# State scans on one Trainium2 core: D products at every second state, and three of four B chunks as products in one step of four instead of in half of the steps

## The reference

```
def step(h, inp):
    x_t, dt_t, B_t, C_t = inp
    A_bar = jnp.exp(dt_t[..., None] * A)
    h = A_bar * h + dt_t[..., None] * B_t[:, None, :] * x_t[..., None]
    y_t = jnp.einsum('bdn,bn->bd', h, C_t)
    return (h, y_t)
...
return y + D * x
```

## Time and profile before

| | us |
|---|---|
| median of 3 runs | 686.62 |
| lowest, highest | 686.56, 692.63 |
| span of the profiled execution, first to last instruction | 657.3 |
| TensorE busy in it | 602.7 |
| VectorE busy | 530.2 |
| ScalarE busy | 513.7 |
| GpSimd busy | 429.1 |

### The profile page before, as it was taken

The page is one execution under the profiler, slowest core; times in us unless marked ns, Lnnn a source line. Parts: engine busy times, 40 slices in busy tenths (PEclk is TensorE's granted clock), DMA queues, the critical chain, the costliest instruction groups (busy, mean ns, idle before and its releaser), DMA issues.

```text
span 657.3 us, 12812 instructions
## 1 busy us (share of the span) xinstructions
PE 602.7 (92%) x4540; PEld 501.7 (76%) x4543; DVE 530.2 (81%) x899; ACT 513.7 (78%) x1182; POOL 429.1 (65%) x261
## 2 busy tenths in 40 slices
PE   5898999999996569799999999999999999999992
PEld 3388999999996434599999999989677555555662
DVE  6798999999998789989999999987863566555374
ACT  2999999999995798899999999967544665444335
POOL 0037999999999302479999999995004277777403
PEclk8979999999999699999999999999999999999997
DMA  7022333333331000044544454438112133333173
GB/s 198 6 67 65 112 112 105 108 109 114 103 110 32 2 0 7 19 147 134 180 128 153 145 159 155 147 91 274 43 64 65 33 97 97 97 99 96 56 265 128
DMA packets 41596, 67.78 MB, mean 103 GB/s; under 512 B 6688, under 2 KB 20928, under 8 KB 41536
## 3 DMA queue, kind: packets, MB, share of 16 engines
q1 hardware_dynamic: 37696, 56.50, 27.5%
q0 software_dynamic: 3840, 10.49, 5.1%
HBM read 57.28 MB, written 9.70 MB: 102 GB/s over the span
## 4 chain that ended last, share of the span: by engine, by line
PE 57%; DVE 14%; ACT 13%; POOL 8%; DMA 4%; issue 3%; DVEq 1%; SPq 0%; ACTq 0%; POOLq 0%
PE both L1383 16%; PE bank L1412 12%; POOL arena L1184 7%; PE both L1476 7%; PE both L1385 5%; PE both L1463 4%; PE bank L1483 4%; DMA arena<-w 2%; ACT rings L1045 2%; PE bank L1404 2%; DVE arena L658 2%; DVE st L443 1%; PE bank L1584 1%; ACT rings L923 1%; ACT tok_a L996 1%
## 5 line engine op out<-in xcount | busy, mean ns | idle before, releaser
L1184 POOL TENSOR_TENSOR arena<-arena,rings 128x1024 f32<-128x1024 f32 x126 | 296.8, 2375 | 17.5 <-DVE arena L658 13.4
L1383 PE MATMUL both<-rings,tok_a 128*128 128x128 f32 x1280 | 183.3, 277 | 3.6 <-DVE arena L658 2.2
L1383 PEld LDWEIGHTS both<-rings,tok_a 128*128 128x128 f32 x1280 | 164.6, 193 | 5.1 <-issue 2.9
L658 DVE TENSOR_TENSOR_SCAN arena<-rings,both 128x1024 f32<-128x1024 f32 x64 | 145.3, 2279 | 12.3 <-PE both L1385 4.5
L658 DVE TENSOR_TENSOR_SCAN arena<-late,both 128x1024 f32<-128x1024 f32 x62 | 140.7, 2278 | 7.1 <-PE both L1385 1.8
L1412 PE MATMUL bank<-ident,arena 128*128 128x128 f32 x1024 | 133.0, 273 | 2.8 <-POOL arena L1184 1.4
L1412 PEld LDWEIGHTS bank<-ident,arena 128*128 128x128 f32 x1024 | 115.7, 141 | 4.2 <-POOL arena L1184 1.9
L1045 ACT ACTIVATE rings<-ident,b_tok 128x128 f32<-128x128 f32 x320 | 106.6, 394 | 0.3
L1045 ACT ACTIVATE rings<-tok_a,b_tok 128x256 f32<-128x256 f32 x192 | 89.7, 500 | 0.0
L1385 PE MATMUL both<-ident,rings 128*128 128x128 f32 x384 | 84.0, 273 | 0.0
L1199 POOL TENSOR_TENSOR arena<-arena,feat_a 128x512 f32<-128x512 f32 x8 | 19.4, 2425 | 86.2 <-DVE arena L554 86.2
(11 more groups left out here) (233 smaller groups left out, 1045.9 us busy)
## 6 DMA issues: line engine op xcount, KB each, us to landing
rings<-c_rows SPq DMA_DIRECT2D x128, 256.0 KB, 3.2
w_sb<-w SPq DMA_DIRECT2D x18, 352.0 KB, 4.2
arena<-w SPq DMA_DIRECT2D x2, 2048.0 KB, 13.2
residual<-x SPq DMA_DIRECT2D x4, 512.0 KB, 5.8
x_rows<-tok_a SPq DMA_DIRECT2D x4, 512.0 KB, 2.6
tok_a<-y_tok SPq DMA_DIRECT2D x4, 512.0 KB, 6.3
w_sb<-y_tok SPq DMA_DIRECT2D x4, 512.0 KB, 7.0
out<-residual SPq DMA_DIRECT2D x8, 256.0 KB, 2.6
```

The costliest lines, as they stand in the source:

```text
L658: dve.tensor_tensor_scan(h_s, decay_s.rearrange("p h t -> p (h t)"), both[s % B_RING][:, :], 0.0, ALU.mult, ALU.add).then_inc(h_ready, 1)
L1184: pool.tensor_tensor(h_both, h_both, c_row, ALU.mult).then_inc(hc_ready, 1)
L1383: pe.matmul(o, tok_a[:, c, h * P:(h + 1) * P], v_ring[:, s % V_RING, j, 0:P], start=True, stop=True)
```

## The change

`diagonals(s)` gives 3 where s is divisible by four and 2 elsewhere, so 16 steps of 64 have three diagonals, not 32. The D products move from n = 1 to 8 to the odd n from 1 to 15, chunk and half in the same order. Rings, waits and transfers stay as they are.

```diff
--- before.py
+++ after.py
@@ -1398,8 +1398,8 @@
                         pe.wait_ge(utr_copied, (l + 1) * Q * 2)
                     if s == 2:
                         pe.wait_ge(d_ready, (l + 1) * H)
-                    if 1 <= n <= H * CQ:
-                        j, h = divmod(n - 1, H)
+                    if n % 2 == 1:
+                        j, h = divmod(n // 2, H)
                         c = b * CQ + j
                         pe.matmul(y_part(b, j, h), feat_a[:, h, c * P:(c + 1) * P], d_diag[:, h, :], start=False, stop=False,
                                   skip_group_check=True)
@@ -1635,7 +1635,7 @@
 
 def diagonals(s):
 
-    return 2 if 1 <= batch_state(s)[1] <= 2 * CQ else 3
+    return 3 if s % 4 == 0 else 2
 
 
 class Tile:
```

## The result

| | before | after |
|---|---|---|
| median of 11 runs each, us | 687.5 | 683.79 |
| lowest, highest | 686.5, 694.51 | 678.18, 690.09 |
| span of the profiled execution | 657.3 | 682.6 |

What follows compares the result with a forecast made beforehand. TensorE was taken to pace much of the scans before, ScalarE all of them after, at 9.59 us per four steps. Gains of 1.65 and 2.55 us, 4.2 together, take the span from 657.3 to 653.1; plus 29.3, 682.4 us, range 680.8 to 687.0.

Steps and rivals of the forecast that it cites:

- ScalarE's 4.848 and 4.740: In the scans: ScalarE's time for a pair with two diagonals per step, and with a single diagonal more.
- The dearer chunks: In the scans: 16 diagonals a layer become whole chunks, 1.7 us more ScalarE work a layer, absorbed by a 2.70 lead.
- Rival A: In the scans: TensorE is the only bound, 32 fewer instructions a layer pay in full; 7.0 us gained, 679.6; 7%.
- the rule that the prediction quotes for it: Trainium skill, Perfetto Trace Analysis: improve the engine with the highest occupancy first, TensorE by its weight loads.
- rival B: In the scans: short step not handed on, four steps cost 9.72, not 9.59; 0.6 us gained, 686.0; 22%.
- rival C: In the scans: ScalarE's 1.7 us a layer come on top, its queue ending with the scan; 690.1; 6%.
- rival D: In the scans: the clock falls to its lower level as products become transposes; over 800 us; 1%.
- all along: In the scans: the profile after would show even scans waiting for ScalarE throughout.
- Layer 1 was to give 2.55 us: Layer 1's scan: scan 62 at 430.3 against 432.86, more than layer 0 because TensorE lost more there.
- Behind both scans nothing changes: After each scan: the last product, sum and transfers start from the scan's end, so nothing else is gained or lost.
- that distance is kept: Whole kernel: the profiled execution stays 29.3 us shorter than the median, so span 653.1 gives 682.4 us.
- within 1%: Whole kernel: time changes by at most 6.9 us either way; given 91%.

Runs made afterwards that it cites:

- scalar_light: Against the kernel after: from step 8 on decays computed for only 384 of 512 tokens, result not the reference's; ratio 0.9908 to the kernel before.
- all_two: Against the kernel after: two diagonals in every step, D products still at odd n; ratio 1.001 to the kernel before.
- before_again: The kernel before, run again with no edit for a second profile; median 661.45 us, ratio 1.0002.
- before_third: The kernel before, no edit, run on a third chip; ratio 0.9991.
- after_again: The changed kernel, no further edit, run again against the kernel before; ratio 0.9963.
- after_third: The changed kernel, no further edit, run on a third chip against the kernel before; ratio 0.9965.

## Why the prediction was right in the scans and wrong in the size

**Right, and shown.** TensorE's 0.110 us for each instruction and 9.49 for four steps (scalar_light: 9.49). ScalarE's 4.848 and 4.740 (all_two: 9.70; after: 9.59). That ScalarE paces the scan and that TensorE stands 0.1 us behind. The sum from decays to scan: 142.4 forecast, 142.30 measured. Layer 0 gained 1.7 us (144.03 less 142.30) where 1.65 stood. The dearer chunks cost ScalarE nothing beyond its lead. Rival A fell with all_two, which takes more instructions from TensorE and whose scans are 1.5 us longer; the rule that the prediction quotes for it, with TensorE taken by its weight loads, does not even point at TensorE, which by them has 76% in the earlier trace rows against VectorE's 81 and ScalarE's 78; rival B with the alternating decays, 4.74 and 4.84; rival C with the lead used up just as the sum had it; rival D with a clock of 1.00 from the decays of step 4 to scan 62 in every profile.

**A cost left out.** VectorE was counted with 8.9 us in four steps. From step 36 to step 56 it also has the statistics, and its sum is 9.37, so that the even scans do not wait for ScalarE "all along". It is still under 9.59, so the time did not change by it.

**A term mis-sized.** Layer 1 was to give 2.55 us. The kernel's part in this is 1.75: before_again and before_third have 144.03 there and after_again and after_third 142.28, while the row taken as the base came from an execution with a low clock. The prediction read the difference between the layers as a loss of TensorE that the change would win back. The loss was that execution's, and 0.7 of its 0.9 us had been gained ahead of the stretch; that the change wins back a TensorE late against ScalarE is borne out by after_third. What the scans gain is 3.5 us, 0.5%, where the sum had 4.2. In the two executions first compared scan 62 of layer 1 came 3.94 us earlier (432.86 and 428.92), near the 4.2, and that is luck in part: 0.34 of it lies ahead of step 4 in layer 0, 1.71 and 2.64 in the scans, and 0.75 was lost between them.

**The step that failed: "Behind both scans nothing changes" and "that distance is kept".** The prediction put everything outside the scans at nothing, and on this gave 91 in 100 to "within 1%" and 6 to faster by more; the measured change was 1.09% (0.82 to 1.36), 7.5 us where 4.2 stood. It carried over the 29.3 us between the profiled execution and the median without asking what they were. About 27 of them were pauses in the expert stage, absent in that one profile. The forecast of the time survives, since the pauses are in the kernel before as in the one after (134.3 and 133.0 us of expert stage). But the chances don't: they stood on a time that differs from execution to execution only by the scans. The stages outside them vary by as much as the change is worth or more. From the last half scan of layer 0 to the first of layer 1 it was 75.9 us in before_third and 79.0 in after_third, with a clock low for 6.8 and 3.4 us at 235.6 and 276.5; from scan 62 of layer 1 to the first L1584 it was 75.1 to 77.5 us in six profiles of the two kernels; the expert stage lasted 130.0 to 134.3 us in the eight profiles that have the pauses. On this floor a gain of 3.5 us in the scans gave ratios of 0.9963, 0.9965 and, the first time, 0.9891.

**What stays open.** The first comparison's 7.5 us are 4 more than the scans explain, and its interval doesn't reach the two later ratios. A part of the difference is which times the ratio counts: the medians of all eleven are 3.71 us apart, about what the scans give, the means 5.0, and the interval about the means reaches the later two. How much of the rest is the changed kernel's doing on that chip is not shown. The two profiles don't show it: from scan 62 of layer 1 to the first L1584 they differ by 0.6 us (75.7 and 75.1). That stretch varies by 2 us by chance, as before_third has 77.5 there with a 3.4 us fall of the clock. Nor is the cause of the pauses known: the rows show TensorE's semaphores late by up to 4 us with its products issued, on two of three chips.

## What to carry to other kernels

Where two engines trade work by a choice in each step, add up what a period costs each engine, with all that it does in that stretch, and choose the mix by the dearer one: of the mixes tried the best is the one whose two sums lie closest (9.59 and 9.49), and taking more from the busiest engine than that costs time (all_two, 9.70). Short overloads behind which the other engine is slower are carried by the rings, so a stretch costs less than its own sum.

Before a median is hung on one profiled execution, compare that execution's span with a timed run's: here 2 us was the usual distance and 29 meant pauses that the one profile lacked, and a change worth less than such stalls vary can come out at twice its size (1.09% where the scans give 0.5) or below it (0.35). A gain in one stage is also no gain of the whole until the next one has been looked at: the diagonals alone won 3.5 us in the scans and lost 9 to 12 behind them (ratios of 1.0074 and 1.0129).

## What was unexpected of the hardware

- In the expert stage TensorE's completions came up to 4 us late (products issued by 570.98, and the copy that waits for them starts at 575.36), with the other engines waiting. Nine of the nineteen distances from pair to pair were over 6.5 us in the kernel after; without pauses they are 5.2 to 5.6, but for a first of 6.1. It was so on two of the three chips on which the experiments ran; the four profiles of the third have none. It made the same kernel 661 us long on one chip and 690 on another.
- A VectorE operation on four columns took 3.01 us beside GpSimd's additions, up to their end (three profiles of three), and 0.25 to 0.27 in the other ten, at the same place behind the first addition.
- A gap of 2.50 us of TensorE was followed by 24 us at half the clock (by 13.7 and 3.4 us on another chip); filling it with idle transposes kept the clock at 0.93 over that stretch.
